# Nine blocks of a dequantised feed-forward layer take a quarter of their inputs as whole numbers

## What is computed

```python
w[k, n] = q[k, n] * s[g, n] - (z[g, n] + 1) * s[g, n],  g = k // 128
gate = x2 @ Wg          # 512 inputs = four groups, 1376 outputs
up = x2 @ Wu
inter = gate * jax.nn.sigmoid(gate) * up
out = (inter @ Wd).astype(jnp.float16)
```

## Time and profile before

| | |
|---|---|
| median of 3 runs | 803.87 us (802.72 to 805.54) |
| the profiled execution, its own time | 808.16 us |
| its span | 806.3 us |
| mean granted TensorE clock over the span | 0.907 |
| PE busy | 689.0 us (85%) |
| DVE busy | 685.0 us (85%) |
| ACT busy | 469.9 us (58%) |

### The profile page before, as it was taken

The page is one execution under the profiler, slowest core; times in us unless marked ns, Lnnn a source line. Parts: engine busy times, 40 slices in busy tenths (PEclk is TensorE's granted clock), DMA queues, the critical chain, the costliest instruction groups (busy, mean ns, idle before and its releaser), DMA issues. The chain is left out here.

```text
span 806.3 us, 8451 instructions
## 1 busy us (share of the span) xinstructions
PE 689.0 (85%) x2794; PEld 326.7 (41%) x2794; DVE 685.0 (85%) x697; ACT 469.9 (58%) x805; POOL 481.4 (60%) x252
## 2 busy tenths in 40 slices
PE   7979889987787799456646889999999999999995
PEld 7623333322122233111111224444444556887885
DVE  6879999999999989999999998999275575585778
ACT  5478768885656765867664546767235346323333
POOL 2429999999999999999999970220002014341130
PEclk9989979999788899856865988999999999999998
DMA  7533232335503705730334409973040030000011
GB/s 234 121 106 136 82 118 76 118 130 168 197 4 117 246 29 170 228 131 26 105 130 150 131 1 249 259 199 93 1 157 1 1 105 0 1 1 1 0 53 52
DMA packets 42358, 83.19 MB, mean 103 GB/s; under 512 B 6825, under 2 KB 10340, under 8 KB 42060
## 3 DMA queue, kind: packets, MB, share of 16 engines
q1 hardware_dynamic: 42316, 82.67, 32.4%
HBM read 71.44 MB, written 11.21 MB: 103 GB/s over the span
## 5 line engine op out<-in xcount | busy, mean ns | idle before, releaser
L2397 POOL TENSOR_TENSOR dbu<-rep_du,bc 128x1024 f32<-128x1024 f32 x127 | 296.5, 2361 | 2.5 <-DMA bc<-bc_scratch 1.2
L1889 ACT ACTIVATE psum<-rep_dt,aneg 128x512 f32<-128x512 f32 x256 | 166.3, 682 | 117.8 <-DVE hc L1239 96.3
L1228 DVE TENSOR_TENSOR_SCAN psum<-psum,dbu 128x1024 f32<-128x1024 f32 x89 | 203.3, 2285 | 3.0 <-ACT psum L1889 1.6
L979 PE MATMUL psum<-hc,stk 128*32 128x512 f32 x512 | 84.6, 743 | 54.5 <-POOL hc L2406 39.7
L1239 DVE TENSOR_TENSOR hc<-psum,bc 128x1024 f32<-128x1024 f32 x89 | 108.9, 1224 | 3.1
L2406 POOL TENSOR_TENSOR hc<-hc,bc 128x1024 f32<-128x1024 f32 x39 | 91.9, 2356 | 9.9 <-DVE hc L1228 9.9
L1228 DVE TENSOR_TENSOR_SCAN hc<-psum,dbu 128x1024 f32<-128x1024 f32 x39 | 88.9, 2280 | 5.5 <-PE psum L979 4.3
L718 PE MATMUL psum<-xf_hi,gu_hi 128*128 128x512 f16 x176 | 66.7, 379 | 0.1
L718 PE MATMUL psum<-xf_hi,gu_lo 128*128 128x512 f16 x176 | 66.7, 379 | 0.0
L718 PE MATMUL psum<-xf_lo,gu_hi 128*128 128x512 f16 x176 | 66.7, 379 | 0.0
L718 PE MATMUL psum<-xT,w_g 128*128 128x512 f32 x120 | 59.1, 641 | 2.6 <-ACT rep_du L2034 2.6
(11 more groups left out here) (301 smaller groups left out, 1455.2 us busy)
## 6 DMA issues: line engine op xcount, KB each, us to landing
rep_dt<-rep_scratch SPq DMA_DIRECT2D x60, 256.0 KB, 3.5
rep_du<-rep_scratch SPq DMA_DIRECT2D x60, 256.0 KB, 4.4
cw<-c_scratch SPq DMA_DIRECT2D x11, 768.0 KB, 8.1
qw<-qgu_in SPq DMA_DIRECT2D x11, 512.0 KB, 6.2
bc<-bc_scratch SPq DMA_DIRECT2D x16, 256.0 KB, 4.8
rep_scratch<-du_t SPq DMA_DIRECT2D x14, 256.0 KB, 2.0
rep_scratch<-dt_t SPq DMA_DIRECT2D x14, 256.0 KB, 2.3
qw<-qd_in SPq DMA_DIRECT2D x11, 256.0 KB, 7.1
```

The lines of the kernel that those rows point to most:

```text
L979: last = pe.matmul(y_rows(k), stk[:], hc[:, (i + k // 2) % HCS, k % 2, :], start=False, stop=(s == GN - 1))
L1228: dve.tensor_tensor_scan(h, a, dbu[:, i % DBS].rearrange("p e t -> p (e t)"), 0.0, ALU.mult, ALU.add)\
L1889: last = act.activation(psum[:, 2 * (i % 2) + e, :], rep_dt[:, cc % 2, k, :], ACT.Exp, scale=aneg[:, k, c, n:n + 1])
L2397: pool.tensor_tensor(dbu[:, i % DBS], rep_du[:, cc % 2, k:k + 2, :], bc[:, n, :].unsqueeze(1).broadcast_to([P, 2, L]), ALU.mult).then_inc( ...
```

## The change

For batch 1's blocks 1 to 9 the last group of inputs (the fourth 128) is no longer multiplied with `gu_hi` and `gu_lo`. Its weights are kept as whole numbers less their zero points (`ints`, exact in float16), their product with the tokens' high and low halves takes two matmuls in place of three and goes into bank 4 (`group_part`), ACT scales it by the group's scale, one number for each partition, into `sg` for the gate and into `it` for the up product (`group_scaled`), and DVE adds the rest of the product from its bank (`gate_sum`, `up_sum`). `silu` then reads and writes `sg` in SBUF (`ffn_silu_sum`), and the product of gate and up is a third DVE instruction (`times_sum`). Blocks 0 and 10 of batch 1 and all of batch 0 stay as they were.

The whole numbers are copied out of the staging slots by nine DMAs from SBUF to SBUF, 64 KB each (`keep_ints`), queued on SP between the loads of the stages; from block 6 on a slot is loaded again only when the copy out of it has landed. Two more DMAs fetch the scales with one number for each partition (`group16`). The two reductions of the attention's weights (`wqkv`, `bqkv`) and a cast of the scales now stand ahead of batch 1's first block on DVE.

```diff
+            def keep_ints(i):
+                sp_.wait_ge(q16_used, i + 1)
+                sp_.dma_start(ints[i][:], cw[i % SLOTS][:, 0, 2 * (KH - 1) * P:2 * KH * P]).then_inc(ints_kept, 16)
             def stage_again(i):
+                if i > SLOTS:
+                    sp_.wait_ge(ints_kept, 16 * (i - SLOTS))
                 sp_.wait_ge(wlo_gu, i - SLOTS + 1)
...
             stage(3)
+            keep_ints(1)
             for i in range(SLOTS, IC):
                 stage_again(i)
+                if i > SLOTS:
+                    keep_ints(i - SLOTS + 1)
+            sp_.wait_ge(ints_kept, 16 * (IC - SLOTS))
+            keep_ints(IC - 3)
...
+            keep_ints(IC - 2)
+            for j in range(2):
+                sp_.dma_start(group16[:, j, :], sgu_in[2 * (KH - 1) + j:2 * KH - 1 + j, :]
+                              .rearrange("r (i n) -> n (r i)", n=P),
+                              allow_slow_non_contiguous=True).then_inc(ld_group, 16)
...
+                def group_part(i, j):
+                    if i > 1 or j:
+                        pe.wait_ge(group_done, 2 * (i - 1) + j)
+                    else:
+                        pe.wait_ge(ints_kept, 16 * (IC - 2))
+                    w = ints[i][:, j * P:(j + 1) * P]
+                    pe.matmul(psum[:, Y_BANK, :], w, xf_hi[1][:, KH - 1, :], start=True, stop=False)
+                    pe.matmul(psum[:, Y_BANK, :], w, xf_lo[1][:, KH - 1, :], start=False, stop=True)\
+                        .then_inc(group_ready, 1)
...
-                        for kk in range(KH):
+                        for kk in range(KH - 1 if grouped else KH):
...
+                        if grouped and j == 0:
+                            group_part(i, 0)
                         product(item, parts).then_inc(work_ready, 1)
+                        if grouped and j == 1:
+                            group_part(i, 1)
...
+            def gate_sum(i):
+                k = IC + i
+                item = ("g", 1, i)
+                wait_work(dve, item)
+                dve.wait_ge(group_done, 2 * i - 1)
+                dve.tensor_tensor(sg[:, k % 2, :], bank(item), sg[:, k % 2, :], ALU.add).then_inc(taken_sem(item), 1)
+            def up_sum(i):
+                k = IC + i
+                item = ("u", 1, i)
+                wait_work(dve, item)
+                dve.wait_ge(group_done, 2 * i)
+                dve.tensor_tensor(it[:, k % 2, :], bank(item), it[:, k % 2, :], ALU.add).then_inc(taken_sem(item), 1)
+            def times_sum(i):
+                k = IC + i
+                dve.wait_ge(silu_done, i)
+                wait_taken(dve, ("u", 1, i))
+                dve.tensor_tensor(it[:, k % 2, :], sg[:, k % 2, :], it[:, k % 2, :], ALU.mult).then_inc(it_done, 1)
...
+            def group_scaled(i, j):
+                k = IC + i
+                if i == 1:
+                    act.wait_ge(group_set, 1)
+                act.wait_ge(group_ready, 2 * (i - 1) + j + 1)
+                if j:
+                    act.wait_ge(itlo_done, k - 1)
+                act.activation((it if j else sg)[:, k % 2, :], psum[:, Y_BANK, :], ACT.Identity,
+                               scale=group32[:, j, i:i + 1]).then_inc(group_done, 1)
...
+                if b == 1 and 1 <= i < IC - 1:
+                    if i - 1 not in (0, 2, 5, 6, 8):
+                        group_scaled(i, 0)
+                        group_scaled(i, 1)
+                    ffn_silu_sum(i)
...
                 if b == 1:
+                    if i in (2, 5, 6, 8):
+                        act.preload_act_table_set(LOG_EXP)
+                    if i == 8:
+                        root(("moe", 0), NT)
+                    if i in (0, 2, 5, 6, 8):
+                        group_scaled(i + 1, 0)
+                        group_scaled(i + 1, 1)
```

More of the change, by code:

```diff
@@ L302, in build @@
         cs = [at(f"cs{s}", STG[s] + 12, [SZ], F16) for s in range(AHEAD)]
+        ints = {i: at(f"ints{i}", 35 + (i - 1) / 2 if i < 9 else 21.25, [2 * P], F16)
+                for i in range(1, IC - 1)}
+        group16 = at("group16", 206.625, [2, IC], F16)
+        group32 = at("group32", 206.75, [2, IC])
         q16 = [at("q16_0", 149, [SZ], F16), at("q16_1", 203, [SZ], F16)]
@@ L451, in build @@
         it_done = sem("it_done")
+        silu_done = sem("silu_done")
+        ints_kept = sem("ints_kept")
+        group_set = sem("group_set")
+        group_ready = sem("group_ready")
+        group_done = sem("group_done")
+        ld_group = sem("ld_group")
         ithi_done = sem("ithi_done")
@@ L682, in _ @@
             load(moe_w["wr"][0][:], wr_dram.rearrange("(k p) n -> p k n", p=P), ld_moe[0])
+            sp_.wait_ge(ints_kept, 16 * (IC - 2))
             sp_.wait_ge(wlo_gu, IC)
@@ L1008, in down @@
                     last.then_inc(ffn_used, 1)
+                def group_part(i, j):
[7 more added lines that the diff above has]
+                        .then_inc(group_ready, 1)
                 for i in range(IC):
                     k = b * IC + i
+                    grouped = b == 1 and 1 <= i < IC - 1
                     if b == 0:
@@ L1498, in att_scores @@
                 link(dve.tensor_reduce(smax[:], sc[:], AX.X, ALU.max))
+                if b == 0:
+                    gate_sum(6)
                 dve.tensor_tensor(sc[:], sc[:], smax[:].unsqueeze(3).broadcast_to(full), ALU.subtract)\
@@ L1507, in att_values @@
                 dve.tensor_reduce(num[:], sc[:], AX.X, ALU.add)
+                if b == 0:
+                    gate_sum(7)
                 link(dve.reciprocal(den[:], den[:]))
@@ L1529, in between @@
                 if i == 1:
-                    ffn_inv16(b)
-                    ffn_add16(b, 0)
-                    ffn_add16(b, 1)
+                    if b == 0:
+                        ffn_add16(b, 1)
+                        ffn_add16(b, 2)
+                    else:
+                        ffn_inv16(b)
+                        ffn_add16(b, 0)
+                        ffn_add16(b, 1)
                 if i == 2:
-                    ffn_add16(b, 2)
+                    if b:
+                        ffn_add16(b, 2)
                     ffn_add16(b, 3)
@@ L1600, in _ @@
                     scaled(i + 3)
+            dve.wait_ge(ld_att, 16 * 7)
+            dve.tensor_reduce(wqkv[:, :, 0:DH], wqraw[:], AX.X, ALU.add).then_inc(wq_done, 1)
+            dve.tensor_reduce(bqkv[:, 0:DH], bqraw[:], AX.X, ALU.add).then_inc(wq_done, 1)
+            dve.wait_ge(ld_group, 32)
+            dve.tensor_copy(group32[:], group16[:]).then_inc(group_set, 1)
             for i in range(IC):
+                if 1 <= i < IC - 1 and i not in (6, 7, 8):
+                    gate_sum(i)
                 if i == IC - 1:
                     low_moe(0, [2, 3])
-                ffn_times(1, i)
+                if 1 <= i < IC - 1:
+                    up_sum(i)
+                    if i == 1:
+                        ffn_inv16(0)
+                        ffn_add16(0, 0)
+                    times_sum(i)
+                else:
+                    ffn_times(1, i)
                 if i == 9:
@@ L1609, in _ @@
                 ffn_low(1, i)
[L1610 to L1613, removed]
                 if i < 8:
@@ L1616, in _ @@
                 if i == 7:
+                    gate_sum(8)
                     between(0, 8)
@@ L2190, in ffn_silu, with ffn_silu_sum @@
                 act.activation(sg[:, k % 2, :], bank(item), ACT.Silu).then_inc(taken_sem(item), 1)
+            def group_scaled(i, j):
+                k = IC + i
+                if i == 1:
+                    act.wait_ge(group_set, 1)
[4 more added lines that the diff above has]
+                               scale=group32[:, j, i:i + 1]).then_inc(group_done, 1)
+            def ffn_silu_sum(i):
+                k = IC + i
+                wait_taken(act, ("g", 1, i))
+                act.activation(sg[:, k % 2, :], sg[:, k % 2, :], ACT.Silu).then_inc(silu_done, 1)
             def ffn_high(k):
                 b, i = divmod(k, IC)
-                wait_taken(act, ("u", b, i))
+                if b == 1 and 1 <= i < IC - 1:
+                    act.wait_ge(it_done, i)
+                else:
+                    wait_taken(act, ("u", b, i))
                 if k >= 2:
@@ L2226, in _ @@
                 b, i = divmod(k, IC)
-                ffn_silu(k)
+                if b == 1 and 1 <= i < IC - 1:
+                    if i - 1 not in (0, 2, 5, 6, 8):
+                        group_scaled(i, 0)
+                        group_scaled(i, 1)
+                    ffn_silu_sum(i)
+                else:
+                    ffn_silu(k)
                 if k == 0:
@@ L2282, in _ @@
                         root(("atto", 0), NT)
-                    if i == 8:
-                        root(("moe", 0), NT)
                     if i in (3, 4):
```

2 lines of the change are left out of this document (removed).

## The result

| | before | after |
|---|---|---|
| median of 5 runs | 803.87 us | 811.79 us (809.78 to 814.37) |
| the profiled execution, its own time | 808.16 us | 814.04 us |
| its span | 806.3 us | 812.1 us |
| batch 1 of the layer in the trace | 120.32 us | 127.50 us |

The ratio is 1.0095, with a 95% interval of 1.0071 to 1.0119: slower by 7.9 us. Later the changed kernel was timed once more, against 17 runs of before: 811.55 to 804.93 us, ratio 1.0079 (1.0048 to 1.0111). The measured time lies in the forecast's range of 804.5 to 812.8; the forecast itself was 809.6 us, +5.7.

A forecast was written before the change was run, and what follows sets the result against it. PE, running without a gap through both batches of the layer, was taken as the bound. Saving -3.9, waits +7.3, clock +2.3 and copies 0 gave +5.7 us, from 803.87 to 809.6 us, range 804.5 to 812.8.

The forecast's parts named there:

- The saving: PE, batch 1: nine blocks lose two matmuls each, 18 times 0.216 us, 3.9 us less.
- The waits: PE waiting on ACT's scalings and DVE's sums in batch 1: 7.3 us in all.
- the four places named: PE's waits: block 4 (0.8 us), block 5 (0.9), block 8 (about 1.3) and block 9 (4.3).
- The chain: DVE and ACT, from DVE's start on qkv to block 9's scaling: 28.5 us grows to 31.8.
- The clock: Behind block 9's gap PE's granted clock falls to half: 2.3 us added, nothing if it holds, 2.9 at most.
- rival of a clock that holds: PE's clock stays full through block 9's gap: +3.4 us, 807.3 us; chance 0.2.
- The 1.3 us gap: PE's wait at block 8 for ACT's scaling, about 1.3 us, with nothing added for the clock.
- The moved reductions: Two reductions moved into DVE's 6.5 us idle time ahead of batch 1's first block: cost nothing.
- The copies: Nine copies on SP between stage loads: 0 us, upper bound 1.5; 8.1 us per stage, about 1 us in hand.
- rival of late loads: Stage loads on SP come late behind copies and DVE holds PE by 1 to 2 us: 811 to 812; chance 0.08.
- rival of hidden additions: The DVE and ACT relay hides the added instructions, so the 18 saved matmuls show: 800.0 us; chance 0.08.
- The total: Whole kernel: +5.7 us, median from 803.87 to 809.6 us, profiled execution from 808.16 to 813.9.

The follow-up runs named there:

- blocks_1_5: Changed kernel with only batch 1's blocks 1 to 5 grouped, 6 to 9 as before the change; 804.72 us against 805.05 before, ratio 0.9997.
- blocks_1_5_9_again: Second run of the changed kernel with only blocks 1 to 5 and 9 grouped; 807.83 us in one run, against 804.93 before.
- blocks_6_9: Changed kernel with only blocks 6 to 9 grouped, 1 to 5 as before the change; 810.51 us against 805.05 before, ratio 1.0064.
- fixed scale: Changed kernel with the scaling's column of scales replaced by one fixed number, 0.002; 814.51 us in one run, against 805.51 before.
- after_again: The changed kernel unaltered, timed and profiled once more; 811.55 us against 804.93 before, ratio 1.0079.
- blocks_12357: Changed kernel with only blocks 1, 2, 3, 5 and 7 grouped; 802.81 us against 805.51 before, ratio 0.9969.

## Why the prediction was right, and where it was off

- **The saving**: as counted, 18 matmuls at 0.216. `blocks_1_5` shows its sum with two waits come to nothing.
- **The waits**: 7.3 us predicted, 8.0 measured, in the four places named, and 0.3 in a fifth, block 7's second group, which the prediction did not have. By brackets they read 1.08, 0.70, 1.43 and 4.18, 7.4 in all, which flatters the estimate. The 0.7 us is block 4's (0.8 predicted, 1.24: its scaling ended 0.3 later than reckoned and PE came 0.1 earlier) and block 8's (1.3, 1.59).
- **The chain**: 31.8 us to the end of the scaling, predicted; 32.3 measured (627.13 to 659.46). The sums had been put at 0.65 and are 0.61. Against that, block 6's second scaling stands ahead of the exponential and was not counted (0.6), and the up sum holds the product by 0.80, not 0.7. The sum is short by 0.5, nearly all of it the missing scaling. PE's waits behind this chain, put at 5.65 us in all, are 6.24 with block 7's (0.30, 1.59, 4.35). `blocks_1_5_9_again` leaves one term of it, 1.7 both predicted and measured.
- **The clock**: taken at 2.3 us, with 2.9 as the upper bound. It is 2.9 in the first trace, 2.5 in `blocks_6_9`, 1.7 with the fixed scale and 1.5 in `after_again`: the size varies by execution, and 2.3 was a fair middle. The half clock lasted 6.8 us in the first two and 3.4 us in the other two, and the part of it that fell into the gap cost nothing. The rival of a clock that holds is out in all four; in these traces it held where the gap was filled or was 2.3 us or less. What lies between 2.3 and 4.3 us no run shows.
- **The 1.3 us gap leaves the clock alone**: so it was.
- **The moved reductions**: free as argued, and worth 0.35 us that the view of waits did not show in before.
- **The copies**: 0, as taken. The cycle of a stage was 8.4 us ((543.46 - 509.85) / 4 between the issues of stages 6 and 10), not 8.1, and stage 10's load, issued at 544.69 and landed 6.6 later, was there 0.5 us before DVE unpacked it at 551.78, where I had left 1 us. I had taken a copy to land 0.3 us behind the load ahead of it: of the first six in the trace after none landed ahead of its load, five landed 0.1 to 0.3 behind, and one 1.2. DVE waits for a DMA between 515 and 560 in one of 14 traces (fixed scale, 0.65 us ahead of block 10's unpacking), and no gap of PE follows. So the mechanism of the rival of late loads exists, but it is too short to reach PE; the longer late loads are at stages 2 to 4.
- **The rival of hidden additions** is out for blocks 6 to 9 by the waits, and holds for blocks 1 to 3, where the added instructions cost PE 0.07 us.
- **The total**: +5.7 forecast, +7.9 and +6.6 measured by medians, +7.2 and +5.8 by batch 1 of the traces. The terms that were short are the waits, by 0.7 us and block 7's 0.3, and in the first trace the clock by 0.6. The rest is within what two sets of medians differ. That the profiled execution took 814.04 us where 813.9 was forecast is luck: its batch 1 is 1.5 us longer than forecast, and its other stages were 1.3 us shorter than those of the profiled execution of before.

So the waits of the changed kernel come from the written order, not from the amount of arithmetic: where DVE and ACT have slack, the change saves more than it costs (`blocks_12357`).

## What to carry to other kernels

Before giving work to engines that only relay, find the one stretch where their chain is as long as the dense engine's work beside it, and count every instruction that the order puts into that stretch, on both relaying engines. A saving spread evenly over blocks can be taken in the blocks with slack and left in the others: five blocks of nine gave a gain where nine gave a loss of three times its size. And read a wait from start to start: the bracket leaves out what the modelled end covers, and here waits of up to 0.3 us have none.

## What the hardware showed that I had not expected

The granted clock fell to half at or behind the 32 matmuls of 128x48 in three of fourteen traces. One of them is of the kernel before, with no gap of PE ahead of it. It came back after 3.4 us each time, which costs 1.7. In the other traces the same instructions passed at full clock. What decides it was not found. The clock's loss behind the same gap of 4.3 us was between 1.5 and 2.9 us. And a delay of PE by the clock can hide a wait that a chain on other engines would have caused, so that a single trace can show a chain as harmless.
